# Attention block and MLP on one core: the pieces of the largest scores in another order, and the end of the setup rearranged

## The reference

```
mod = silu(condition) @ Wada + bada                # six vectors for each batch entry
xm  = layernorm(x) * (1 + sc_a) + sh_a
qkv = xm @ Wqkv
scores = where(causal, q k^T * hd**-0.5, -inf)     # 1024 x 1024 for each of 8 x 16 heads
x   = x + gt_a * (softmax(scores) @ v @ Wproj + bproj)
xm  = layernorm(x) * (1 + sc_m) + sh_m
x   = x + gt_m * (gelu(xm @ W1 + b1) @ W2 + b2)
```

## Time and profile before

| what | us |
|---|---|
| median of 3 runs (lowest to highest) | 3441.56 (3436.78 to 3441.98) |
| the profiled execution | 3438.84 |
| its span, first to last instruction | 3437.1 |
| granted TensorE clock over the span, share of full speed | 0.981 |
| PE busy / DVE busy / POOL busy / ACT busy | 3234.3 / 2066.9 / 1554.4 / 1166.6 |

### The profile page before, as it was taken

One profiled execution on the slowest core, in us unless ns is written; L12 is line 12 of the kernel. 1 busy time (PEld: TensorE's weight loads), 2 busy tenths in 40 slices (PEclk: granted clock), 3 DMA queues, 4 the chain that ended last, 5 costly groups with the idle time before them and its releaser, 6 DMA issues.

```text
span 3437.1 us, 70538 instructions
## 1 busy us (share of the span) xinstructions
PE 3234.3 (94%) x25708; PEld 2595.2 (76%) x25708; DVE 2066.9 (60%) x2511; ACT 1166.6 (34%) x2322; POOL 1554.4 (45%) x1312
## 2 busy tenths in 40 slices
PE   7789999999999999998839999999999999999999
PEld 4566666666666666665539999899899899899998
DVE  5476776677677667666355555555555555555552
ACT  2145555555555555556511121111111111111111
POOL 2145666665566665577753233333333333333332
PEclk9999999999999999999969999999999999999999
DMA  5545555555555555565441222222221222221220
GB/s 210 162 142 166 177 162 166 173 160 175 172 171 163 171 172 154 175 188 159 113 127 53 59 67 58 58 66 59 58 69 56 58 70 55 58 72 53 58 61 13
DMA packets 303514, 391.88 MB, mean 114 GB/s; under 512 B 24240, under 2 KB 206000, under 8 KB 303336
## 3 DMA queue, kind: packets, MB, share of 16 engines
q1 hardware_dynamic: 289904, 367.84, 37.5%
q10 hardware_dynamic: 13440, 21.50, 1.8%
HBM read 270.66 MB, written 118.06 MB: 113 GB/s over the span
## 4 chain that ended last, share of the span: by engine, by line
PE 81%; DVE 12%; issue 4%; ACT 2%; DMA 1%; SPq 0%; DVEq 0%; POOL 0%; ACTq 0%
PE psH L853 21%; PE psY L866 21%; PE psA L674 9%; PE psT L715 6%; PE psA L752 5%; DVE mx L1158 5%; PE psP L832 5%; PE psA L670 4%; PE psS L690 3%; DVE psS L1154 3%; PE psA L725 3%; DVE xin L1110 1%; PE psA L643 1%; PE psP L842 1%; ACT e L935 1%
## 5 line engine op out<-in xcount | busy, mean ns | idle before, releaser
L1399 POOL TENSOR_TENSOR h_l<-h_full,h_h 128x256 fp32r<-128x256 f32 x512 | 489.0, 955 | 1121.4 <-DVE h_h L1319 1121.4
L935 ACT ACTIVATE e<-psT 128x512 f32<-128x512 f32 (+1 forms) x1202 | 605.3, 555 | 632.8 <-PE psT L715 631.3
L1439 POOL TENSOR_TENSOR es<-e 128x1024 f32<-128x1024 f32 (+1 forms) x320 | 624.4, 1951 | 404.6 <-PE psA L725 233.9
L1158 DVE TENSOR_REDUCE mx<-psS 128x4 f32<-128x2048 f32 (+3 forms) x384 | 666.4, 1756 | 229.9 <-PE psS L690 224.4
L1033 ACT ACTIVATE h_full<-psH,b1c 128x256 f32<-128x256 f32 x512 | 243.9, 476 | 1332.8 <-PE psH L853 1332.8
L853 PE MATMUL psH<-a_h,w1p_h 128*128 128x256 f32 x2048 | 578.2, 282 | 7.5 <-DVE a_l L1314 7.5
L853 PE MATMUL psH<-a_h,w1p_l 128*128 128x256 f32 x2048 | 580.8, 284 | 0.0
L853 PE MATMUL psH<-a_l,w1p_h 128*128 128x256 f32 x2048 | 580.4, 283 | 0.0
L1319 DVE CAST h_h<-h_full 128x256 fp32r<-128x256 f32 x512 | 148.7, 290 | 539.8 <-ACT h_full L1033 538.6
L715 PEld LDWEIGHTS psT<-qst,kst 97*128 97x128 f32 x2404 | 354.8, 192 | 119.2 <-issue 70.1
L715 PE MATMUL psT<-qst,kst 97*128 97x256 f32 (+1 forms) x2404 | 412.8, 292 | 11.7 <-ACT e L935 11.7
(11 more groups left out here) (113 smaller groups left out, 4771.1 us busy)
## 6 DMA issues: line engine op xcount, KB each, us to landing
qk_split<-qk_hl SPq DMA_DIRECT2D x128, 512.0 KB, 3.4
kst<-qk_split SPq DMA_DIRECT2D x128, 256.0 KB, 4.0
qst<-qk_split SPq DMA_DIRECT2D x128, 256.0 KB, 4.1
xin<-in_x_dram SPq DMA_DIRECT2D x64, 256.0 KB, 4.4
values<-vout ACTq DMA_DIRECT2D x64, 256.0 KB, 3.7
kmx<-qk_split SPq DMA_DIRECT2D x32, 512.0 KB, 4.6
qmx<-qk_split SPq DMA_DIRECT2D x32, 512.0 KB, 5.9
kst<-qk_split SPq DMA_DIRECT2D x128, 128.0 KB, 3.9
```

Of the source, the lines that this page charges most:

```text
L935: act.activation(e[:, s % ERING, 2 * hp:2 * hp + 2, 0:w], score_bank(s, hp, with_a)[:, :, 0:w], ACT.Exp, scale=SCALE).then_inc(sem("exp_do ...
L1158: reduce = dve.tensor_reduce(mx[:, part, :, qt], psS[:, :, col:col + w], AX_X, ALU.max)
L1399: return pool.tensor_tensor(dst, full, high.bitcast(F32), ALU.subtract)
L1439: pool.tensor_tensor(to, first, second, ALU.add).then_inc(sem("added"), 1)
```

## The change

- **Order of the pieces.** The plain pieces (4,0), (5,0), (6,0) become pieces 0, 1, 2. Behind them come double, single, double, single, double, and last the plain (7,0). The work of the nine pieces together is the same.
- **SP.** `store_modulation(2, 6)` and the loads of the first group's `kmx` and `qmx` move from behind all stores of block 1 to behind the store of its item 8. `load_max` waits only for the stores in the ring slot of the group that it loads, where it had waited for all four slots.
- **DVE and POOL.** Block 3 is no longer normalised at item 3 of block 2. Its statistics and aggregation come at the end of block 1, POOL's `a_rstd` and DVE's `normalise` at item 0 of block 2.
- **Pieces in the setup.** They stand behind the items 1 to 9 of block 2. `max_join`, `max_turn`, `max_row` and `place_max` of the first group, which stood before item 11, come behind it, and on DVE behind the splits of block 3.
- **Body 0.** PE forms the first half of block 3's item 0 (6 matmuls) ahead of the first scores. It had followed them.

```diff
 MAXES = (
-    (((0, 0, 0, 128), (2, 0, 0, 384)), slice(0, 4, 3)),
-    (((1, 0, 0, 256), (5, 1, 512, 256)), slice(1, 4, 2)),
-    (((4, 1, 512, 128), (6, 1, 512, 384)), slice(0, 4, 3)),
-    (((3, 0, 0, 512),), slice(3, 4)),
     (((4, 0, 0, 512),), None),
     (((5, 0, 0, 512),), None),
     (((6, 0, 0, 512),), None),
+    (((0, 0, 0, 128), (2, 0, 0, 384)), slice(0, 4, 3)),
+    (((7, 1, 512, 512),), slice(3, 4)),
+    (((1, 0, 0, 256), (5, 1, 512, 256)), slice(1, 4, 2)),
+    (((3, 0, 0, 512),), slice(3, 4)),
+    (((4, 1, 512, 128), (6, 1, 512, 384)), slice(0, 4, 3)),
     (((7, 0, 0, 512),), None),
-    (((7, 1, 512, 512),), slice(3, 4)),
 )
...
# SP, in the loop over the stores of blocks 0 and 1
                     a_store(ia, n)
+                    if ia == 1 and n == A_NV + IPB:
+                        store_modulation(2, 6)
+                        sp.wait_ge(sem("mod_stored"), 32)
+                        sp.wait_ge(sem("mod_turned"), 6)
+                        load_max(0, 0)
...
# SP, load_max
-                for s in range(QK_RING):
+                for s in (hg,) if isinstance(u, int) else range(QK_RING):
                     sp.wait_ge(qk_stored[s], (b + 1) * (2 * A_NQK // QK_RING * 16))
...
# PE, body
+                    ahead = u == 0 and s == 0
+                    if ahead:
+                        a_item(AHEAD, *item_at(0), False, with_ln)
                     for hp in range(2):
                         scores(u, s, hp, with_a)
...
-                    if at and not late:
+                    if at and not late and not ahead:
...
# PE, setup
-                        if n < NMX:
-                            max_item(0, 0, n)
+                        if 0 < n <= NMX:
+                            max_item(0, 0, n - 1)
                     if n in TURN_AFTER_ALONE:
                         a_turn(ia + 1, TURN_AFTER_ALONE.index(n), True)
-                    if ia == AHEAD - 1 and n == A_ITEMS - 2:
-                        max_turn(0, 0)
+            max_turn(0, 0)
...
# ACT, setup
-                    if ia == AHEAD - 1 and n == A_ITEMS - 1:
-                        place_max(0, 0, 1)
                     a_copy(ia, n, True)
...
+            place_max(0, 0, 1)
             body(0, True, True, False, 0)
...
# DVE, setup
-                    if n == 3:
+                    if n == 3 and ia < AHEAD - 1:
                         layer_norm(ia + 1)
+                    if n == 0 and ia == AHEAD - 1:
+                        for r in range(NXR):
+                            normalise(AHEAD, r)
...
-                        if n < NMX:
-                            max_item(0, 0, n)
-                        if n == A_ITEMS - 2:
-                            max_join(0, 0)
-                            max_row(0, 0)
+                        if 0 < n <= NMX:
+                            max_item(0, 0, n - 1)
                 a_split(ia + 1, KT - 1)
+                if ia == AHEAD - 2:
+                    for r in range(NXR):
+                        ln_stats(AHEAD, r)
+                    ln_aggregate(AHEAD)
+            max_join(0, 0)
+            max_row(0, 0)
...
# POOL, setup
-                    if n == 3:
+                    if n == (3 if ia < AHEAD - 1 else 0):
                         a_rstd(ia + 1)
```

More of the change, by code:

```diff
@@ L406, in o_store @@
                   .then_inc(o_stored[n % 2], 16)
[L409 to L418, removed]
             def load_rows(u, ahead, p, kind, tile, cols, done):
@@ L469, in load_v @@
                 sp.dma_start(vst[:, ahead % 2], src[:, :, bass.ds(hg * P, P)]).then_inc(v_loaded[ahead % 2], 16)
-            sp.wait_ge(sem("mod_stored"), 32)
-            sp.wait_ge(sem("mod_turned"), 6)
-            load_max(0, 0)
+            store_modulation(0, 2)
+            for r in range(NXR):
+                load_x(1, r)
+            for ia in range(2):
+                for n in range(A_NV, A_ITEMS):
+                    if n == A_NV + 3:
+                        for r in range(NXR):
+                            load_x(ia + 2, r)
+                    a_store(ia, n)
+                    if ia == 1 and n == A_NV + IPB:
[3 more added lines that the diff above has]
+                        load_max(0, 0)
             load_k(0, 0, 0)
@@ L1223, in _ @@
                             dve.wait_ge(sem("masks_ready"), 1)
-                        if n < NMX:
-                            max_item(0, 0, n)
-                        if n == A_ITEMS - 2:
-                            max_join(0, 0)
-                            max_row(0, 0)
-                a_split(ia + 1, KT - 1)
+                        if 0 < n <= NMX:
+                            max_item(0, 0, n - 1)
+                a_split(ia + 1, KT - 1)
+                if ia == AHEAD - 2:
+                    for r in range(NXR):
+                        ln_stats(AHEAD, r)
+                    ln_aggregate(AHEAD)
+            max_join(0, 0)
+            max_row(0, 0)
             body(0, True, True, False)
```

## The result

| | us |
|---|---|
| changed kernel, median of 4 runs (lowest to highest) | 3384.93 (3384.44 to 3387.04) |
| kernel before, median of 4 runs | 3440.69 (3436.78 to 3441.98) |
| ratio, 95% interval | 0.9841 (0.9824 to 0.9858) |
| span of the profiled execution, before and after | 3437.1 and 3383.3 |
| granted TensorE clock over the span, before and after | 0.981 and 0.988 |

The change saves 55.8 us by the medians and 53.8 us between the two profiles. The work is the same. The page of the changed kernel shows it: as many reductions and masks at nearly the same mean durations. VectorE (DVE) is idle less before the masks (172.3 us where it was 231.0).

A forecast was written before the change was run, and what follows sets the result against it. PE was taken as the bound almost everywhere, so only its idle or lower-clock time could be won. Setup 16 + ends 24 + middles 5.4 + clock 7 - bodies 13 to 15 1.4 = 51.0 us, giving 3390.5, range 3378 to 3411.

The forecast's parts named there:

- The load: Setup, block 2: `qmx` is there near 124, PE asks at about 131, so the 9.02 us wait goes.
- The waits in block 2: Setup: PE waits 4.9 us in all behind block 2's pieces; item 11 starts at 169.1, 16.6 us gained.
- The join behind the splits: Setup, from item 11 to the scores: 10.0 us where it was 3.0, a loss of 7.0; scores near 179.1.
- The end of a body: End of bodies 0 to 11: PE waits shrink, 2.0 us gained each, bounds 1.0 and 2.4; 24 us for 12.
- The danger: Body ends: moved splits may fall on other POOL work; one subtraction took 0.69 us alone, 1.66 beside a POOL instruction.
- The middle of a body: Middle of 12 bodies: waits of 0.94 and 0.22 go, partly returning; 0.45 us each, bounds 0 and 1.1, 5.4 in all.
- The clock: Behind body ends: the five cases of lower clock go, 5 x 1.4 = 7 us, bounds 0 and 7.
- Bodies 13 to 15: Last bodies' attention: masked pieces wait wherever they stand; 1.4 us slower over five groups, bounds -4 and +4.
- Moved waits (B): Rival, bodies: waits move with the masks to pieces 4, 6 and 8, the clock keeps falling; 3412, chance 0.14.
- E: Rival, slower: double pieces at r = 1, 5 and 9 fully exposed, 3.7 us in a group; 3467, chance 0.03.
- C: Rival, setup alone: the bodies come out even, only the setup's 16 us is gained; 3425.5, chance 0.07.
- D: Rival, setup's cover gone: row's DMA or splits take longer than 7 us, setup gives 5; 3401.5, chance 0.06.

The follow-up runs named there:

- load_early: The kernel before with SP's part alone, the earlier modulation store and first group's loads: one run, 3427.26 us against 3438.41 beside it.
- pool_short: The changed kernel with GpSimd's additions of neighbouring exponentials cut to 16 columns, the rest of the sums left out: one run, 3358.96 us.
- order_only: The kernel before with the new order of the pieces and nothing else: median 3395.52 us, ratio 0.9867.
- setup_only: The changed kernel with the old order of the pieces: median 3432.46 us, ratio 0.9971 against the kernel before.
- double_third: The changed kernel with pieces 2 and 3 exchanged, so the first double comes one place earlier: one run, 3408.97 us.
- join_early: The changed kernel with the first group's join, turn and row ahead of item 11 again, first scores ahead of block 3's item 0: median 3379.43 us.
- row_first: The changed kernel with SP's first loads of body 0 held until the first scores are formed: one run, 3384.97 us.

## Why the prediction was right, step by step

The direction, the mechanism and the sum held: 3390.5 forecast, 3384.93 measured. That the sum came so near is in part luck. The ends gave 9.2 us less than forecast and the middles 9.6 us more, and these two misses cancel; so do the setup's 2.9 less and the 3.4 more of bodies 13 to 15.

- **The load.** Right. PE does not wait for `qmx`, and load_early showed 11.0 us where the wait of 9.02 and the clock behind it were to go.
- **The waits in block 2.** Forecast 1.2, 1.4, 0.35, 1.1 and 0.8; measured 1.09, 1.30, 0.15, 1.15 and 0.91. Item 11 began near 168.6, forecast 169.1.
- **The join behind the splits.** The 7.0 us was too small; it was 9.1 (12.1 us from the start of item 11 to the scores, where it had been 3.0). Scores came 3.9 us after the row's DMA was issued, not 2.4, since the first loads of body 0 stood ahead of it. So they began at 180.65 and not 179.1. After that the granted clock was 0.87 over body 0's first group, and from its first piece to its turn it took 37.5 us where the steps gave 34.7. The turn came at 218.83, where the steps gave 214.9 and I had allowed 1 us for the clock. 13.1 us instead of 16.
- **The end of a body.** The mis-sized term. I took 2.0 us, it was 1.2: the first split ahead of piece 1 was as forecast, but the second and third ended at 870.3 where I had them end 1.7 us earlier. The danger was named, and with the bound that came out nearly (1.0). pool_short showed that it is GpSimd's additions, and both waits of PE went with them.
- **The middle of a body.** Mis-sized the other way: 1.25 us each, not 0.45, and above the upper bound of 1.1. I expected the turn of the next block to wait 1 us behind the longer piece 3. It waited 0.43. The last normalisation took 0.54 us, while I had reckoned with the 0.94 it had taken before. In the timeline before, an addition of GpSimd runs beside it (956.95 to 959.36, the normalisation from 958.69); in the changed kernel the addition ends at 922.45 and the normalisation starts at 922.99. That this is why it is shorter is argued; no run tests it.
- **The clock.** Right, 6.9 of 7 us. order_only and setup_only tie it to the order and not to the new setup, double_third to the long wait.
- **Bodies 13 to 15.** Forecast 1.4 us slower, measured 2.0 faster. The first of the five intervals, at full clock in both kernels, grew from 40.46 to 41.90 us: the forecast loss is there. But over all five the granted clock is 0.98 where it was 0.96. In the profiles they sum to 195.2 to 196.8 us with the new order (the changed kernel twice, order_only, join_early, row_first) and to 195.6, 197.9 and 201.9 with the old one (load_early, before, setup_only, at 0.97, 0.96 and 0.93). So the sign rests on where the lower clock falls, and what decides that stays open.
- **The rivals.** Moved waits (B) did occur: 1.22 and 0.60 us came back of 2.21 + 0.22 + 0.30, but the doubles at r = 5 and 9 show no wait in the loop, as the intervals of 4.3 and 4.9 us behind them had promised for the 4.2 that they need. That also rules out E. C falls with order_only, which gains 46.1 us with the old setup, and D with the 13.1 us of the setup, where it had 5.

## What to carry to other kernels

Where one buffer passes between two engines, the order of unequal pieces is worth as much as their sum: put the short ones where the consumer has other duties, the long ones where the producer has more than their time. Ask of each duty on the waited-for engine when its result is first needed. A split that stood one piece too early cost 1.4 us at each of 12 body ends. And a step that is moved gets a new queue ahead of it: the join behind four splits gave back half of what the rest of the change had won by the first scores (8.0 of 16.1 us against join_early), and 4.9 of 18.0 by the end of the first group.

## What the runs showed of the hardware

- GpSimd's additions lengthen DVE's fp32 cast of 128x512 from 0.42 to 1.22 us and a subtraction with two inputs in SBUF from 0.69 to 1.78 us. One of a body's four subtractions took 1.66 us beside an addition in the kernel before, too. The Trainium skill (GPSIMD Engine Reference, Key points) states that the two share SBUF interfaces; the trace agrees and gives the price. In the kernel before, the split's casts in bodies 0 to 11 took 0.47 us at most, in the changed kernel up to 1.22: a reordering that changes no instruction changed their length.
- Behind a PE wait of 2.2 us at a body's end the granted clock fell to the lower level (1.2 GHz) for a few microseconds at 5 of 12 places (6 of 12 in load_early) and cost 1.4 us each time. Behind 2.49 us (double_third) it fell at 11 of 11 and cost 1.6 to 3.1 us, and behind 1.22 us at none of 12. The same wait of 2.2 us did it at some ends and not at others, so its length is not the whole condition.
- An 8 KB DMA on ACT's queue landed 1.9 us after its issue with one store of 512 KB in flight, and 3.8 us with loads of up to 256 KB issued from 0.7 us ahead of it on SP's queue as well.
